# Planning a turn further ahead on SyncE, and adding the masks of a graph attention by 24 narrow matmuls in front of the scores

## What is computed

```
Q = x @ WQ.T;  K = x @ WK.T;  V = x @ WV.T
attn = Q @ K.T * 32 ** -0.5 + (Q @ we.T + be)
attn = attn + where(adj > 0, 0, -inf);  attn = softmax(attn)
hard = (attn == max(attn)) / 8
out = hard @ V                      # heads side by side, 4096 x 256
result = layernorm(x + out)
```

## Time and profile before

| | |
|---|---|
| median of 3 runs | 1508.6 us |
| the profiled execution, time / span | 1507.79 us / 1506.0 us |
| prologue, until the first item's scores | about 170 us |
| loop over 50 turns | about 1300 us, 6.5 us an item |
| granted PE clock, mean of the span | 0.906 |
| busy: PE, PEld, DVE, ACT, POOL | 71, 50, 68, 54, 49% |

### The profile page before, as it was taken

One profiled execution on the slowest core, in us unless ns is written; L12 is line 12 of the kernel. 1 busy time (PEld: TensorE's weight loads), 2 busy tenths in 40 slices (PEclk: granted clock), 3 DMA queues, 4 the chain that ended last, 5 costly groups with the idle time before them and its releaser, 6 DMA issues.

```text
span 1506.0 us, 45736 instructions
## 1 busy us (share of the span) xinstructions
PE 1075.3 (71%) x12346; PEld 750.5 (50%) x12347; DVE 1017.3 (68%) x3051; ACT 807.3 (54%) x1483; POOL 732.7 (49%) x820
## 2 busy tenths in 40 slices
PE   5778477776777777777776776677676776777771
PEld 3333355554555555555554554555555555555551
DVE  5445377777767776777777676777677677767771
ACT  2333265565646566656665655656556556654550
POOL 0000455666556555555565555544545445545650
PEclk9989699899989999989999999998989889898995
DMA  4643466566656666667666666766766767655650
GB/s 168 217 154 126 150 224 208 174 184 213 181 195 179 207 218 221 185 208 212 224 193 199 210 212 193 220 213 199 242 215 198 222 216 231 202 177 148 186 173 28
DMA packets 89473, 290.94 MB, mean 193 GB/s; under 512 B 16944, under 2 KB 30000, under 8 KB 89456
## 3 DMA queue, kind: packets, MB, share of 16 engines
q0 software_dynamic: 48720, 199.60, 43.1%
q1 hardware_dynamic: 40736, 91.15, 18.1%
HBM read 275.98 MB, written 14.71 MB: 193 GB/s over the span
## 4 chain that ended last, share of the span: by engine, by line
PE 31%; issue 22%; DVE 11%; ACT 9%; DMA 7%; DVEq 6%; SPq 6%; another core or an unknown queue 5%; POOL 1%; ACTq 1%; POOLq 1%
PE ps_s L1153 9%; PE ps_s L1172 5%; DMA kv<-kv_table,picks 4%; PE ps_h L1164 3%; PE ps_s L1089 3%; DVE best L901 2%; PE ps_s L1155 2%; ACT hard L617 2%; ACT masked L606 2%; ACT joined L575 2%; ACT k_t L612 2%; SPq L388 2%; PE ps_o L1184 2%; PE ps_s L1079 2%
## 5 line engine op out<-in xcount | busy, mean ns | idle before, releaser
L516 POOL DMA_INDIRECT kv<-kv_table,picks x609 | 584.3, 959 | 335.0 <-PE ps_o L1184 166.7
L1153 PE MATMUL ps_s<-k_t,q_blk 128*128 128x384 f32 x804 | 392.2, 573 | 37.9 <-ACT masked L606 30.3
L507 POOL TENSOR_TENSOR q_blk<-q_t,minus_same 128x256 f32<-128x256 f32 x202 | 146.9, 727 | 401.3 <-issue 197.7
L602 ACT ACTIVATE hard_t<-ps_h 128x768 bf16<-128x768 bf16 x200 | 162.1, 811 | 302.6 <-remote 151.9
L612 ACT COPY k_t<-ps_s 128x384 f32<-128x384 f32 x404 | 177.0, 482 | 182.3 <-PE ps_s L1172 150.8
L901 DVE TENSOR_REDUCE best<-ps_s 128x1 f32<-128x384 f32 x402 | 210.3, 549 | 90.9 <-PE ps_s L1155 65.6
L617 ACT ACTIVATE hard<-ps_s,minus_top 128x384 bf16<-128x384 f32 x402 | 211.3, 581 | 74.9 <-DVE minus_top L906 53.9
L1172 PE MATMUL ps_s<-ident_f,kv 128*128 128x128 f32 x1212 | 182.3, 290 | 45.3 <-DMA kv<-kv_table,picks 26.2
L1155 PEld LDWEIGHTS ps_s<-mask_of,masked 128*128 128x128 bf16 x1206 | 110.2, 105 | 169.3 <-issue 123.9
L1164 PE MATMUL ps_h<-ident_b,hard 128*128 128x128 bf16 x1200 | 112.5, 236 | 90.3 <-ACT hard L617 57.9
L1140 PE MATMUL ps_x<-pay,reached 128*128 x1224 | 118.4, 233 | 75.1 <-issue 66.9
(11 more groups left out here) (138 smaller groups left out, 1197.3 us busy)
## 6 DMA issues: line engine op xcount, KB each, us to landing
adj_in<-in_adj SPq DMA_DIRECT2D x128, 512.0 KB
kv_table<-kv_out SPq DMA_DIRECT2D x32, 320.0 KB, 2.6
kv<-kv_table,picks POOLq DMA_INDIRECT x609
x_in<-in_x SPq DMA_DIRECT2D x8, 512.0 KB, 6.7
x_row<-in_x SPq DMA_DIRECT2D x32, 128.0 KB
out<-y_out SPq DMA_DIRECT2D x32, 128.0 KB
plan<-places_of SPq DMA_DIRECT2D x208, 0.0 KB
turn_flags<-flags_of SPq DMA_DIRECT2D x52, 0.0 KB
```

What stands on the lines that cost most here:

```text
L516: pool.indirect_dma_start(kv[m % RING][:, c, :], None, kv_table, bass.IndirectOffsetOnAxis(ap=picks[m % RING][:, c, 2:3], axis=0)).then_in ...
L602: act.activation(hard_t[m % 2][:], hard_rows_t, ACT.Copy, bias=1.0).then_inc(act_hard_t, 1)
L1153: pe.matmul(bank[:, 0:SLOTS], q_blk[m % 2][:, h, :], k_t[m % 2][:, h, :], start=True, stop=False)
```

## The change

Two edits, which do not depend on each other.

**SP.** The plan is made at the end of SP's turn instead of between the first and the second quarter's load, and one plan more is made before the loop. So the plan that others take at the end of turn t is sent in SP's turn t - 1, behind its loads and rows. What a plan holds and how others take it stay the same. SP's loop must then run on the flag of a turn earlier (`more_was`).

**Masks.** `masked` holds each chunk's 32 queries once (124 x 96 in all, where it was 124 x 384). A new function `beyond` adds the mask first, for both halves: for each half, chunk and head a matmul with a 128 x 32 stationary operand and 128 moving columns, at the head's 32 partitions. That is 2 x 3 x 4 = 24. `scores` of a half is then the f32 product alone, accumulated on top.

```diff
@@ SP
-            def turn():
-                for k in ("fe", "fe_on", "te_on"):
+            def plan_next():
+                for k in ("fe", "fe_on", "te_on", "more"):
                     sp.reg_mov(r[f"{k}_was"], r[k])
                 sp.reg_mov(r["te_was"], r["te_done"])
-                load_part(0)
                 sp.wait_ge(planned, r["due"])
                 sp.wait_ge(dve_merge, r["n"])
                 for i in range(RING):
                     plan_place(i)
                 plan_turn()
                 planned_turn()
-                for i in range(1, QUARTERS):
+
+            def turn():
+                for i in range(QUARTERS):
                     load_part(i)
                 with sp.If_ne(r["te_on_was"], 0):
                     row = sp.snap(r["te_was"], min_val=0, max_val=T - 2) * P
                     rows(sp.snap(r["te_was"]) & (T - 1), row, False)
+                plan_next()
                 sp.reg_add(r["n"], r["n"], RING)
 
-            run_turns(sp, r, turn)
+            plan_next()
+            run_turns(sp, r, turn, "more_was")
+            sp.wait_ge(planned, r["due"])
@@ ACT
-                act.activation(masked[m % RING][0:USED], bits[m % RING][0:USED].rearrange("p c l k -> p c (l k)")
-                               .unsqueeze(2).to_broadcast([USED, CHUNKS, HEADS4, GQ]), ACT.Relu, bias=one[0:USED],
+                act.activation(masked[m % RING][0:USED], bits[m % RING][0:USED].rearrange("p c l k -> p c (l k)"),
+                               ACT.Relu, bias=one[0:USED],
                                scale=-1.0).then_inc(act_masked, 1)
@@ PE
+            def beyond(m, due):
+                pe.wait_ge(act_masked, due(act_masked))
+                for h in range(HALVES):
+                    for c in range(CHUNKS):
+                        for j in range(HEADS4):
+                            pe.matmul(ps_s[m % 2][h][j * GQ:(j + 1) * GQ, c * P:(c + 1) * P], masked[m % RING][:, c, :],
+                                      mask_of[:], start=(c == 0), stop=False)
+
             def scores(m, due, h):
                 if h == 0:
                     pe.wait_ge(q_made, due(q_made))
-                    pe.wait_ge(act_masked, due(act_masked))
-                bank = ps_s[m % 2][h]
-                pe.matmul(bank[:, 0:SLOTS], q_blk[m % 2][:, h, :], k_t[m % 2][:, h, :], start=True, stop=False)
-                for c in range(CHUNKS):
-                    mm = pe.matmul(bank[:, c * P:(c + 1) * P], masked[m % RING][:, c, :, :].rearrange("p h q -> p (h q)"),
-                                   mask_of[:], start=False, stop=(c == CHUNKS - 1))
-                mm.then_inc(pe_score[h], 1)
+                pe.matmul(ps_s[m % 2][h][:, 0:SLOTS], q_blk[m % 2][:, h, :], k_t[m % 2][:, h, :], start=False, stop=True
+                          ).then_inc(pe_score[h], 1)
@@
                     planes_of(b + 4, for_loop(pe, r, 4), (None, finish_ranks, finish_rank_step, None)[b], f"value{b + 4}")
+                    beyond(b + 1, for_loop(pe, r, 1))
                     scores(b + 1, for_loop(pe, r, 1), 0)
                     hards_across(b, for_loop(pe, r, 0))
                     scores(b + 1, for_loop(pe, r, 1), 1)
```

More of the change, by code:

```diff
@@ L161, in hard_attention @@
         bits = [sb(f"bits{i}", [P, CHUNKS, 2, 16], U32) for i in range(RING)]
-        masked = [sb(f"masked{i}", [P, CHUNKS, HEADS4, GQ], BF16) for i in range(RING)]
+        masked = [sb(f"masked{i}", [P, CHUNKS, GQ], BF16) for i in range(RING)]
         kv = [sb(f"kv{i}", [P, CHUNKS, ROW], F32) for i in range(RING)]
@@ L291, in next_item, with run_turns @@
                 eng.reg_load(r["left"], n_items[P - 1:P, bass.ds(g, 1)])
-        def run_turns(eng, r, turn):
+        def run_turns(eng, r, turn, more="more"):
             with eng.Fori(0, TURNS_OUTER):
-                with eng.If_ne(r["more"], 0):
+                with eng.If_ne(r[more], 0):
                     with eng.Fori(0, TURNS_INNER):
-                        with eng.If_ne(r["more"], 0):
+                        with eng.If_ne(r[more], 0):
                             turn()
@@ L370, in _ @@
                                        "limit", "before0", "before1", "before2", "fe_was", "fe_on_was", "te_was",
-                                       "te_on_was"),
+                                       "te_on_was", "more_was"),
                           n=BASE, fe=FIRST_TILES, fin=FIRST_TILES)
@@ L771, in _ @@
             for i in range(RING):
-                done = dve.tensor_copy(masked[i][:].rearrange("p c h q -> p (c h q)"),
-                                       be_row[:].to_broadcast([P, SLOTS]))
+                done = dve.tensor_copy(masked[i][:].rearrange("p c q -> p (c q)"),
+                                       be_row[:].to_broadcast([P, CHUNKS * GQ]))
             done.then_inc(dve_k, 1)
@@ L1242, in _ @@
                 keys_across(m, for_item(m), 48, m)
+            beyond(0, for_item(0))
             for h in range(HALVES):
```

## The result

| | median | runs |
|---|---|---|
| before | 1507.1 us | 4, from 1503.0 to 1518.3 |
| changed | 1599.9 us | 4, from 1586.1 to 1604.2 |
| ratio | 1.0594 | 95% interval 1.0544 to 1.0644 |

What follows compares the result with a forecast made beforehand. Bound taken as a ring of dependences over four engines, none busy above 71%. SP -15, ACT -12, PE +9 make -18 from 1507.8, giving 1490; 3 us more on SP gives 1487 us, range 1464 to 1512.

Steps and rivals of the forecast that it cites:

- SP, -15 and 3 on top: Plan sent a turn earlier: PE's 15.0 us of plan waits go; 3 us more for POOL and ACT, waiting for the same flags.
- rival C: Another wait, SP's for `counted` or PE's for kv, replaces the plan's; SP gives only -3: 1503 us, chance 0.18.
- ACT, -12: Masks' activation L606 writes 96 elements, not 384: 0.24 us less an item, about -12 us on the path.
- PE, +9: 24 narrow mask matmuls replace six: +0.13 us an item, 26 us busy time, 35% of it on the path, +9 us.
- the 40 that I had named as a sign of error: Prediction called itself wrong if PE's busy time rose by more than 40 us.
- the other price in the prediction: Skill page's least time between matmul starts, about 25 ns: the 24 would take 0.6 us, sum some 10 us higher.
- The step that failed: DVE's merge after `values` (24 matmuls), 0.49 us from first start, taken as evidence beyond the model that column tiles run side by side.
- -18 - 3: Sum of SP -15, ACT -12 and PE +9, with 3 us more put on SP.
- rival A: The forecast itself, all three terms as summed: 1470 to 1507 us, likely 1473 to 1500; chance 0.5.
- Rival D: Slower: the 24 matmuls hold PE longer ahead of half 0, as changes of form drain the array; 1516 to 1552; chance 0.15.
- D's turning point of 0.5 us an item: Extra PE time an item from which D decides: +35 us on the path, +8 after ACT and SP, 1516 us.

Runs made afterwards that it cites:

- six wide masks in front: Kernel before with its six full-width mask matmuls moved ahead of both halves' products: 0.992 of before; with the SP edit added, 0.990.
- plain loads: Each indirect gather replaced by a plain POOL load of 128 rows of the same size: kernel before 1397.4 us, changed kernel 1355.0 us in one set.
- without gathers: Loop's gathers removed, the first four items' K and V rows used for all: kernel before 1389.5 us, changed kernel 1356.6 us.
- 24 full-width ones of 32 columns: Kernel before with six full-width masks in front, each cut into four matmuls of 32 moving columns, no column tiles: 1.055 of before.

## Why the prediction was wrong

- **SP, -15 and 3 on top.** The mechanism held: no wait for `turn_flags` is left, and the plan now lies at the end of SP's turn. The four places take 7.43 us there, and the flags' DMA, 0.65 us, comes behind them at 744.37:

```profile
719.97 12.54 SPq L458 DMA_DIRECT2D adj_in<-in_adj  x4
...
735.88 7.43 SPq L388 DMA_DIRECT2D plan<-places_of  x4
744.37 0.65 SPq L413 DMA_DIRECT2D turn_flags<-flags_of  x1
```

  The worth did not: 0.998 alone. This looks like the pattern of rival C (a wait takes the place of the plan's), with another wait than C named, the late words of PE; that they took its place was not shown; with six wide masks in front the edit gives 0.2% more at most, too.
- **ACT, -12.** 394 ns against 390 forecast, and the waiters fell from 30.3 us, 61 times to 12.0 us, 39 times. Right.
- **PE, +9.** The group of 24 takes 0.52 us and the next product starts 0.44 us behind its first start, both as worked out from `values`. PE's busy time rose by 51 us against 26, past the 40 that I had named as a sign of error; in that kernel the product's own mean rose from 573 to 603 ns. With plain loads, in the profiled executions, it is 1046.5 against 1031.7 us, +15, and without gathers 1043.9 against 1014.1, +30. The matmuls' price in PE's own time was right to within that. (By the starts in the records the tiles follow each other at 13 ns; the 24 full-width ones of 32 columns at 26 ns. A start every 25 ns, the other price in the prediction, would on the footing of my own sum have added 19 us, not 10: I had left out the 0.13 us behind the last start.)
- **The step that failed** is "The record is not only modelled: DVE's merge ... began 0.49 us after the first had started" and all that I built on modelled ends: that a result of PE is with its readers when its record ends. One row was enough to trust it for the kernel before, and it is true where nothing delays. But the kernel before already broke it in half of its items. The `hards_across` of the earlier trace rows ends at 1009.75, and ACT, idle by then for 0.9 us, took its result at 1011.63:

```profile
1011.63 0.81 ACT L602 ACTIVATE hard_t<-ps_h 128x768 bf16<-128x768 bf16 x1 [2.81 <-remote]
```

  That is a delay of 1.9 us, and "another core or an unknown queue" stood at 5% in the earlier trace rows. I gave it no term. It is the largest of the changed kernel: the mean delay grew by 0.9 us, 182 us over 202 items if all of it lay on the path, where the sum had nothing; the sum of all late words doubled, from 679 to 1351 us. The measured change is +93 us against the -21 forecast, and it is -33 to -42 us where no word is late; so lateness made the change dearer by some 130 us. Against plain loads the gathers' form costs the kernel before 8% (1 / 0.926) and the change 19% (1.056 / 0.884; two sets, in which the kernel before took 1528.7 and 1529.8 us).
- **The sum without it.** Where no result is delayed the change gives -33 us (no gathers) and -42 us (plain loads), against my -18 - 3. Its sign was right, its size too small by 12 to 21 us; which term is short was not tried. The granted clock, for which the sum had no term, is one candidate: 0.94 for the change against 0.93 for before without gathers, and 0.94 against 0.92 with plain loads. (The range of rival A was added up too low as well: -5 - 5 + 12 gives 1510, not 1507.)
- **Rival D** had the right side and place, ahead of half 0 and of `hards_across`, and the wrong mechanism. The array's drain between forms, which the page "TensorEngine Tiling (Array Packing)" of the Trainium skill (section "Key Properties") states, shows no price of its own in these runs: 24 full-width matmuls lose as much. D's turning point of 0.5 us an item was not reached on PE, it was passed outside PE.

The Trainium skill's page "Perfetto Trace Analysis" (section "Tensor Engine Instruction (MATMUL, LD_WEIGHTS)") states that the end of a matmul in the profile is an estimate from its size, and that the acknowledgement of its writes and the word to the other engines come after it. The trace agrees: the delays of up to 3.2 us stand in no row of PE. By that page every number of the earlier trace rows that is an end should have been set beside the start of its reader.

**What is shown, and what stays open.** Shown: the loss is the masks' part; it needs the number of matmuls (6 or 24, all else equal) and not column tiles; it needs the indirect gathers on POOL and not their bytes; what is late is PE's semaphores, at ACT, DVE and POOL, and where they are not late the change is faster. Open: what in an indirect gather holds them, and why many short matmuls make it longer. In 102 of the 166 delayed items ACT was let go 0.7 to 1.1 us behind the end of a gather's record, a stretch that holds 18% of the loop's time; that fits a hold by the gather but was only observed. Open, too, why one set of runs has none of it, with the same gathers, and how the changed kernel itself does there: it was not run in it.

## What to carry to other kernels

Set the modelled end of each PE group beside the start of the engine that waits for it, for every such result and not for one, and give the difference a term of its own: where "remote" or "an unknown queue" releases a wait on one core, that time responds to what PE and POOL do and can outweigh every price of an instruction. Replacing few long matmuls by many short ones is not free just because their record is short; while indirect gathers run, count the instructions too. And before a cause is sought, take the suspected disturber out of both kernels: here two runs without it showed that the forecast's own sum had the right sign.

## What the runs showed that I had not expected

- A wait for PE's result that ends late, in the kernel before by over 1 us in 63 of 172 items and by 3.2 us at most. In the changed kernel POOL was let go within 0.4 us of ACT in 141 of the 166 delayed items, and DVE in 87. With plain loads of the same 199.60 MB on the same queue it is gone: 0.04 us in 151 items but one.
- Two sets of runs differ by 7% for the same kernel, 1427.3 us in one and 1506.7 to 1531.2 us in the others; the four kernels profiled in the first show no delays.
- Less work on PE can cost time: where nothing was delayed, the kernel without mask matmuls took 1443.0 us at a mean granted clock of 0.89, before 1427.3 us at 0.92.
- A plain load on POOL is cheaper for POOL as well: its busy time is 480 us with them against 731 us with the indirect ones, at three transfers an item.
- 24 matmuls of 128 columns on column tiles take 0.52 us, so (0.52 - 0.22) / 23 = 13 ns from start to start, the last alone being some 0.22 us.
